# Normalisation statistics of ten feed-forward tiles on ScalarE, and one transpose moved ahead of the MLP's first products

## The chip, the cores and the metric

The kernel runs on one core of one Trainium2 chip. A core has five engines that each run their own list of instructions in order: TensorE (PE in the profile; its weight loads are PEld), VectorE (DVE), ScalarE (ACT), GpSimd (POOL) and SyncE (SP), which issues DMAs. They wait for one another only through semaphores. The metric is the device time of one execution in microseconds, as the median of a few runs; lower is better.

## What is computed

Eight sequences of 256 tokens with 256 features go through one decoder layer: a Mamba block with a gated MLP, an mLSTM cell (the "mixer"), and a feed-forward part whose operands are rounded block by block to a 4-bit grid. Each of the three stands behind a layer norm and a residual. Cut to what the change touches:

```python
def _layernorm(x, axis=-1, eps=1e-05):
    m = jnp.mean(x, axis=axis, keepdims=True)
    v = jnp.var(x, axis=axis, keepdims=True)
    return (x - m) / jnp.sqrt(v + eps)

# Mamba block (inside _L0_attn_ref)
y = y * jax.nn.silu(z)
y = _rms(y, ssm_norm_w)          # x * rsqrt(mean(x*x) + eps) * w
x = x + y @ out_proj_w.T
xn = _rms(x, rms_w)
a, g = jnp.split(xn @ fc1_w.T, 2, axis=-1)
x = x + (a * jax.nn.silu(g)) @ fc2_w.T

# the three sublayers
x = x + _L0_attn_ref(_layernorm(x), ...)
x = x + _L0_xattn_ref(_layernorm(x), ctx, ctx, ...)
x = x + _L0_ffn_ref(_layernorm(x), w_gate, w_up, w_down)

# feed-forward
gate = fp4_linear(x, w_gate)     # quantise x and w in blocks of 16, then matmul
h = jax.nn.silu(gate) * fp4_linear(x, w_up)
out = fp4_linear(h, w_down)
```

## The kernel before

The 2048 rows are 16 tiles of 128 tokens (T = 16), two (C = 2) to each of the B = 8 batches. All work is written out by hand, engine by engine, as lists of stages; a helper `step` calls each stage for the unit that has reached it. Two blocks of code follow each other, `front` (Mamba, MLP, and the query side of the mixer) and `mixer_and_ffn`.

**The front.** A loop over steps k runs with software lags. Two constants matter: SCAN = 9, the step at which the state-space scan starts, and MLP = 18, the step at which the first pair of `fc1` products is issued. Batch numbers in the scan are b = k - SCAN. At k = 18 the scan has only its tail left: batch 7, tile 0 and tile 1 of which still have to be turned (`turn`, four 128x128 transposes on PE into bank 5), copied out by ACT (`turned_y`, line 1151) and projected (`project_out`, line 897). Bank 5 and the target ygT are shared. So `turn(7, 1)` waits for `ygT_ready`, that is, for ACT's `turned_y(7, 0)`. ACT runs `squares` (line 1144, sum of squares with an accumulator) ahead of each `turned_y`, and ahead of both, at k = 18, the two `silu_gate` calls (line 1180) of the first MLP pair. These wait for PE's `fc1` (line 922). `fc1(b, pair)` is 16 weight-load and matmul pairs in the trace (fp32 counts two for each), `fc2` is line 935.

**The feed-forward part.** In `mixer_and_ffn` tile t passes these stages, each at a lag in rounds r:

- ACT `norm(t)` in round t (line 1827, Identity with scale and shift from memory), then DVE's quantiser on x in round t + 1 (lines 320 to 338, tiles xq_*, with ACT's `lift_x`, line 1822, in the middle);
- PE `turn_x` (1701), ACT `turned_x` (1814), PE `gate_up` (1711), ACT `silu` (1808) in round t + 2;
- DVE `product` (1928) and the quantiser on h (tiles hq_*, `lift_h` on ACT, line 1818) in round t + 3;
- PE `turn_h` (1722), ACT `turned_h` (1802, 1803), PE `down` (1730) in round t + 4; DVE `output` (1950) in round t + 5, then the store by SP.

Within a round ACT's order is `turned_x, turned_h, lift_x, lift_h, silu, norm`. PE's is `turn_x, turn_h, gate_up, down`. `gate_up(t)` waits for `turned_x(t)` and for `product(t - 1)`; `product(t)` waits for `silu(t)`. Rounds 0 to 4 are interleaved with the last steps of the mixer; rounds 10 to 15 are a hardware loop of two rounds a pass, on every engine; the others are written out.

**The statistics.** The layer norm ahead of the feed-forward part needs mean and variance of each row. DVE's `row_stats(b)` makes them for both tiles of a batch: two `bn_stats` (line 1918), two `bn_aggr` (line 1922) into `mv`. GpSimd's `row_rstds(b)` makes 1/sqrt(var + eps) and the shift (lines 2027, 2029, 2032), and `norm` waits for that. Batches 0 to 2 are done in mixer steps 4 to 6. Batches 3 to 7 are done between rounds of the feed-forward part: `row_stats(3)` ahead of round 5, and `row_stats(4)` to `row_stats(7)` at the end of rounds 5 to 8.

## Time and profile before

| | us |
|---|---|
| median of 3 runs | 586.91 (586.39 to 587.0) |
| profiled execution, its own time | 588.3 |
| its span, first to last instruction | 586.6 |
| front block | 0 to about 379 |
| mixer, with the first rounds of the feed-forward part from about 415 | 379 to about 450 |
| feed-forward rounds 5 to 15 | about 457 to 554 |
| last rounds | 554 to 586.6 |

The profile is one execution, read by a hardware profiler. For a chain of work that ends late one looks first at which engine has no idle time in a stretch, then at the waits of that engine, then at its rows in order of time. An instruction is pipelined, so that the next one of the same engine often starts about 0.1 us before the end that the row gives; distances between starts are the safer measure. In the last 130 us DVE is nearly without a gap, and in the stretch from 200 to 379 us PE is.

### The profile page before, as it was taken

The page shows a single profiled execution, that of the slowest core. Times are in us where ns is not written, and L with a number is a line of the kernel's source. Part 1 is how long each engine was busy: PE and PEld are TensorE (multiplying, and loading weights), DVE is VectorE, ACT ScalarE, POOL GpSimd, SP SyncE. Part 2 cuts the span into 40 slices and gives each one's busy share as a digit, 9 for nine tenths or more (in the row PEclk, how much of TensorE's full clock was granted, in tenths as well). Part 3 has the DMA queues.
Part 4 walks back from the last instruction along what each step waited for, and adds up shares of the span by engine and source line. Part 5 has one row for each costly group of instructions (what it writes and reads, how often), then busy time and mean ns, then how long its engine had stood idle before and what let it go on. Part 6 is the DMA issues. An engine that isn't in the chain of part 4 may idle for free. (4 is left out here: it accounts for less than half of the span.)

```text
span 586.6 us, 9295 instructions
## 1 busy us (share of the span) xinstructions
PE 559.1 (95%) x3003; PEld 455.6 (78%) x3003; DVE 444.8 (76%) x985; ACT 277.3 (47%) x685; POOL 132.4 (23%) x189
## 2 busy tenths in 40 slices
PE   7999999999999899999999999999997898999995
PEld 6767677689888788888888888878875676777774
DVE  6876799898896234764755856587999999999994
ACT  3876766785796521311111112366874343444431
POOL 4120024454544201211010010007961101000000
PEclk8999999999999999999999999999998899999998
DMA  9300001010000291000000000011000000000000
GB/s 307 128 18 9 29 15 41 7 43 5 6 5 1 87 262 52 1 1 1 0 2 0 1 0 1 4 39 57 19 2 1 10 19 10 18 19 9 18 18 28
DMA packets 21683, 18.94 MB, mean 32 GB/s; under 512 B 12040, under 2 KB 20616, under 8 KB 21256
## 3 DMA queue, kind: packets, MB, share of 16 engines
q1 hardware_dynamic: 21208, 18.36, 9.9%
q8 instruction: 24, 0.39, 0.3%
q14 instruction: 19, 0.16, 0.1%
q10 hardware_dynamic: 432, 0.03, 0.0%
HBM read 16.04 MB, written 2.34 MB: 31 GB/s over the span
## 5 line engine op out<-in xcount | busy, mean ns | idle before, releaser
L922 PE MATMUL ps<-xnT,w_fc 128*128 128x256 f32 x512 | 112.8, 380 | 0.0
L922 PEld LDWEIGHTS ps<-xnT,w_fc 128*128 128x128 f32 x512 | 96.5, 190 | 12.7
L1711 PE MATMUL ps<-w_fc,scores 128*128 128x352 f32 x256 | 81.5, 472 | 3.0 <-issue 3.0
L1711 PEld LDWEIGHTS ps<-w_fc,scores 128*128 128x128 f32 x256 | 48.5, 195 | 29.8 <-issue 5.3
L1180 ACT ACTIVATE xs<-ps 128x512 f32<-128x512 f32 x32 | 19.1, 598 | 95.8 <-PE ps L922 75.7
L1302 DVE SCALAR_TENSOR_TENSOR fold<-xpad,conv_w,fold 128x256 f32<-128x256 f32 x120 | 50.8, 482 | 6.2 <-ACT fold L1082 5.4
L1730 PE MATMUL ps<-u_res,hT 128*128 128x256 f32 x192 | 45.9, 390 | 3.8 <-DVE scores L1950 2.8
L1730 PEld LDWEIGHTS ps<-u_res,hT 128*128 128x128 f32 x192 | 37.5, 196 | 11.9 <-issue 3.0
L799 PE MATMUL ps<-xnT,fold 128*128 128x256 f32 x160 | 39.4, 393 | 1.2 <-ACT xpad L1076 1.2
L799 PEld LDWEIGHTS ps<-xnT,fold 128*128 128x128 f32 x160 | 30.3, 197 | 7.7 <-issue 2.1
L897 PE MATMUL ps<-w_out,xF 128*128 128x256 f32 x128 | 30.4, 381 | 0.8 <-DVE u_res L1401 0.8
L726 POOL TENSOR_SCALAR q_ve<-q_mv 128x2 f32<-128x2 f32 x8 | 1.7, 218 | 129.2 <-DVE q_mv L1426 129.2
L1410 DVE TENSOR_TENSOR fold<-ps,xs 128x512 f32<-128x512 f32 x16 | 11.1, 691 | 26.2 <-ACT xs L1180 26.2
L807 PE MATMUL ps<-fold,xnT 128*128 128x512 f32 x64 | 30.4, 600 | 0.0
L897 PEld LDWEIGHTS ps<-w_out,xF 128*128 128x128 f32 x128 | 23.7, 190 | 7.4 <-issue 4.7
L693 POOL TENSOR_SCALAR_AFFINE_SELECT scores<-scores 128x128 f32<-128x128 f32 x16 | 14.6, 932 | 63.2 <-ACT scores L1110 63.2
L708 POOL TENSOR_TENSOR bc<-xs,head_c 128x512 f32<-128x512 f32 x16 | 25.9, 1623 | 11.8 <-DVE zs L1394 11.8
L935 PE MATMUL ps<-zs,xpad 128*128 128x256 f32 x128 | 28.4, 380 | 0.0
L935 PE MATMUL ps<-zs,fold 128*128 128x256 f32 x128 | 28.3, 379 | 0.0
L935 PEld LDWEIGHTS ps<-zs,fold 128*128 128x128 f32 x128 | 24.3, 190 | 3.3
L935 PEld LDWEIGHTS ps<-zs,xpad 128*128 128x128 f32 x128 | 24.2, 190 | 3.3
L1410 DVE TENSOR_TENSOR xpad<-ps,xs 128x512 f32<-128x512 f32 x16 | 11.1, 692 | 20.1 <-ACT xs L1180 20.1
(305 smaller groups left out, 1202.1 us busy)
## 6 DMA issues: line engine op xcount, KB each, us to landing
zs<-in_ffn_w SPq DMA_DIRECT2D x1, 2112.0 KB, 10.9
x_res<-in_x SPq DMA_DIRECT2D x8, 256.0 KB, 5.8
w_fc<-in_w_fc SPq DMA_DIRECT2D x1, 2048.0 KB, 9.7
xnT<-in_ctxT SPq DMA_DIRECT2D x8, 256.0 KB, 3.1
xs<-in_ctx SPq DMA_DIRECT2D x16, 128.0 KB, 2.9
xs<-in_ctxT SPq DMA_DIRECT2D x8, 256.0 KB, 3.1
out<-scores SPq DMA_DIRECT2D x16, 128.0 KB, 1.7
segs<-segment_rows SPq DMA_DIRECT2D x64, 6.0 KB
```

The costliest lines, as they stand in the source:

```text
L693: last = pool.affine_select(out=tile, in_=tile, pattern=[[1, P]], compare_op=ALU.is_ge, fill=0.0, base=0, channel_multiplier=-1)
L708: pool.tensor_tensor(heads(dx[:, c, :]), heads(m.xs[:, n, :]), inner(m.head_c[:, 2, :], HD), ALU.mult)\
L799: last = pe.matmul(bank[1 + n % 2][:, 0:S], w_in[:, kk, w0:w0 + P], turned_u(b, kk), start=(kk == 0), stop=(kk == KD - 1))
L807: last = pe.matmul(bank[3 + c][:], turned_u(b, kk)[:, c * P:(c + 1) * P], w_in[:, kk, 0:DI], start=(kk == 0), stop=(kk == KD - 1))
L897: last = pe.matmul(bank[6][:, c * D:(c + 1) * D], ygT[:, c, k * P:(k + 1) * P], m.w_out[:, k, :], start=(k == 0), stop=(k == DI // P - 1))
L922: last = pe.matmul(bank[half + r][:, i * S:(i + 1) * S], m.w_fc1[:, kk, col:col + P], m.xnT[:, b, kk * S:(kk + 1) * S], start=(kk == 0), s ...
L935: last = pe.matmul(bank[4 + c][:, 0:D], hid[p][:, k, c * P:(c + 1) * P], w_fc2[:, k, :], start=(k == 0), stop=(k == KM - 1))
L1180: act.activation(gate[:, r, :], bank[2 + r][:], ACT.Silu).then_inc(g["gate_ready"], 1)
L1302: dve.scalar_tensor_tensor(conv[:, p, k, :], xpad[:, p, k, tap:tap + S], m.conv_w[:, ch, tap:tap + 1], conv[:, p, k, :], ALU.mult, ALU.add)\
L1410: dve.tensor_tensor(hid[p][:, 2 * pair:2 * pair + 2, :].rearrange("p k t -> p (k t)"), bank[r][:], gate[:, r, :], ALU.mult).then_inc(g["hi ...
L1711: last = pe.matmul(bank[1 + j][:, 0:HALF], xT[:, p, k * P:(k + 1) * P], m.w_gu[:, k, j * HALF:(j + 1) * HALF], start=(k == 0), stop=(k == ...
L1730: last = pe.matmul(bank[7][:, 0:D], hT[:, p, k, :], m.w_dn[:, k, :], start=(k == 0), stop=(k == KF - 1))
```

## The change

It has two parts that don't touch each other.

**In the front,** at step 18, `turn(7, 0)` is issued on PE ahead of `fc1(0, 0)` and `fc1(0, 1)`; on ACT `squares(7, 0)` and `turned_y(7, 0)` stand ahead of `silu_gate(0, 0)` and `silu_gate(0, 1)`. The argument `n=B - 1` keeps the old place for batches 0 to 6.

**In the feed-forward part,** batches 3 to 7 lose `row_stats` on DVE. ACT gets a `row_stats(t)` for one tile, called for t = r + 2 at the end of rounds 4 to 13. It makes two passes over the 256 elements of a row: Identity with scale 1/256, whose accumulator is the mean, and Square of (mean - x), whose accumulator is 256 times the variance; between the two it waits for its own first pass. GpSimd multiplies by 1/256 where it adds eps, in one instruction as before. ACT's rounds 10 to 15 are no longer a loop but written out.

```diff
@@ front, PE
+            if k == MLP:
+                turn(B - 1, 0)
             on(fc1, k - MLP, 0)
             on(fc1, k - MLP, 1)
-            on(turn, b - 2, 0)
+            on(turn, b - 2, 0, n=B - 1)
@@ front, ACT
+            if k == MLP:
+                squares(B - 1, 0)
+                turned_y(B - 1, 0)
             on(silu_gate, k - MLP, 0)
             on(silu_gate, k - MLP, 1)
-            on(squares, b - 2, 0)
-            on(turned_y, b - 2, 0)
+            on(squares, b - 2, 0, n=B - 1)
+            on(turned_y, b - 2, 0, n=B - 1)
@@ feed-forward, ACT
+        def row_stats(t):
+            b, mean, square_sum = t // C, mv[:, t, 0:1], mv[:, t, 1:2]
+            act.wait_ge(s["x2_ready"], LEAD + C * (b + 1))
+            act.wait_ge(f["f_mv_ready"], LEAD + b)
+            scrap = sq[:].rearrange("p i e -> p (i e)")[:, 0:D]
+            act.activation(scrap, m.x_res[:, t, :], ACT.Identity, scale=1.0 / D, accum_out=mean)\
+               .then_inc(f["f_stats"], 1)
+            act.wait_ge(f["f_stats"], LEAD + STATS_BY_DVE + t + 1 - C * STATS_BY_DVE)
+            last = act.activation(scrap, m.x_res[:, t, :], ACT.Square, bias=mean, scale=-1.0, accum_out=square_sum)
+            if t % C == C - 1:
+                last.then_inc(f["f_mv_ready"], 1)
...
-        rounds(act, forward, 4)
+        for r in range(4, T + depth_of(forward)):
+            step(T, forward, r)
+            if C * STATS_BY_DVE <= r + 2 < T:
+                row_stats(r + 2)
@@ feed-forward, DVE
-            if 4 <= k <= B - 2:
+            if 4 <= k < 4 + STATS_BY_DVE:
                 row_stats(k - 4, k % 2)
...
-        row_stats(3, 1)
-        for r in range(5, 9):
-            step(T, forward, r)
-            row_stats(r - 1, (r - 1) % 2)
-        rounds(dve, forward, 9)
+        rounds(dve, forward, 5)
@@ feed-forward, GpSimd
-            pool.tensor_scalar(ve[:, here], mv[:, here, 1], LN_EPS, None, ALU.add).then_inc(f["f_ve_ready"], 1)
+            pool.tensor_scalar(ve[:, here], mv[:, here, 1], share, LN_EPS, ALU.mult, ALU.add)\
+                .then_inc(f["f_ve_ready"], 1)
```

PE in the front at step 18, the difference between the two kernels (L907 is `turn_xn`, L888 `turn`, L922 `fc1`, L897 `project_out`; fp32 matmuls count once here):

```order
 L897 MATMUL ps<-w_out,xF 128x256 x4
 L907 MATMUL ps<-ident,fold 128x128 x4
+L888 MATMUL ps<-ident,zs 128x128 x4
 L922 MATMUL ps<-xnT,w_fc 128x256 x16
-L888 MATMUL ps<-ident,zs 128x128 x8
+L888 MATMUL ps<-ident,zs 128x128 x4
 L897 MATMUL ps<-w_out,xF 128x256 x8
 L922 MATMUL ps<-xnT,w_fc 128x256 x8
```

The two turnings stood together behind the products; now one stands ahead of them.

ACT at the same step, before (L1172 is `turned_xn`, L1180 `silu_gate`, L1144 `squares`, L1151 `turned_y`):

```order
233 L1172 ACTIVATE xnT<-ps,rms_w 128x256 x2
234 L1180 ACT_TABLE_LOAD
235 L1180 ACTIVATE xs<-ps 128x512 x2
236 L1144 ACTIVATE xF,ms<-zs 128x512
237 L1151 ACTIVATE xF<-ps 128x512
238 L1144 ACTIVATE xF,ms<-zs 128x512
239 L1151 ACTIVATE xF<-ps 128x512
```

and now (two lines further down in the file):

```order
233 L1174 ACTIVATE xnT<-ps,rms_w 128x256 x2
234 L1146 ACTIVATE xF,ms<-zs 128x512
235 L1153 ACTIVATE xF<-ps 128x512
236 L1182 ACT_TABLE_LOAD
237 L1182 ACTIVATE xs<-ps 128x512 x2
238 L1146 ACTIVATE xF,ms<-zs 128x512
239 L1153 ACTIVATE xF<-ps 128x512
```

`squares` and `turned_y` of tile 0 now run ahead of the table load and the two silu calls.

ACT in one feed-forward round, before (L1814 `turned_x`, L1802 and L1803 `turned_h`, L1822 `lift_x`, L1818 `lift_h`, L1808 `silu`, L1827 `norm`):

```order
331 L1814 ACTIVATE scores<-ps 128x256
332 L1802 ACTIVATE hT<-ps 128x512
333 L1803 ACTIVATE hT<-ps 128x256
334 L1822 ACTIVATE xq_g<-xq_g,grid_bias 128x256
335 L1818 ACTIVATE hq_g<-hq_g,grid_bias 128x704
336 L1808 ACTIVATE sg<-ps 128x704
337 L1827 ACTIVATE scores<-x_res,f_shift,f_rstd 128x256
```

and now (six lines further down; L1842 and L1845 are the two passes):

```order
333 L1820 ACTIVATE scores<-ps 128x256
334 L1808 ACTIVATE hT<-ps 128x512
335 L1809 ACTIVATE hT<-ps 128x256
336 L1828 ACTIVATE xq_g<-xq_g,grid_bias 128x256
337 L1824 ACTIVATE hq_g<-hq_g,grid_bias 128x704
338 L1814 ACTIVATE sg<-ps 128x704
339 L1833 ACTIVATE scores<-x_res,f_shift,f_rstd 128x256
340 L1842 ACTIVATE scores,f_mv<-x_res 128x256
341 L1845 ACTIVATE scores,f_mv<-x_res,f_mv 128x256
342 L1820 ACTIVATE scores<-ps 128x256
```

The two passes stand between `norm` and the next round's `turned_x`, with no table load among them.

## Rows read from the trace of the kernel before

**Rows 1.** Page, part 1: busy us, share of the span and instructions of each engine.

```profile
PE 559.1 (95%) x3003; PEld 455.6 (78%) x3003; DVE 444.8 (76%) x985; ACT 277.3 (47%) x685; POOL 132.4 (23%) x189
```

**Rows 2.** Busy time by stretch: PE, PEld, DVE, ACT, POOL, then PE clock, DMA.

```profile
215.00:370.00 155.00, 155.00 (x759) 136.96 (x758) 96.23 (x203) 28.43 (x57) 17.75 (x25) 1.00 0.05 12
```

**Rows 3.** PE's waits, 200 to 385 us: total us, times, longest.

```profile
PE ps L888 <- ACT xF L1151: 1.7, 1, 1.7
```

**Rows 4.** Timeline of step 18: start, duration, engine, line, operation [idle before <-releaser].

```profile
190.86 7.07 PE L922 MATMUL ps<-xnT,w_fc 128*128 128x256 f32 x32
...
194.56 1.28 ACT L1180 ACT_TABLE_LOAD   x1 [2.66 <-PE ps L922]
...
197.77 0.60 PE L888 MATMUL ps<-ident,zs 128*128 128x128 f32 x4
198.03 0.60 ACT L1180 ACTIVATE xs<-ps 128x512 f32<-128x512 f32 x1 [1.58 <-PE ps L922]
198.52 0.62 ACT L1144 ACTIVATE xF<-zs 128x512 f32<-128x512 f32 x1
...
199.33 0.60 ACT L1151 ACTIVATE xF<-ps 128x512 f32<-128x512 f32 x1
...
200.07 0.63 PE L888 MATMUL ps<-ident,zs 128*128 128x128 f32 x4 [1.70 <-ACT xF L1151]
...
200.53 3.62 PE L897 MATMUL ps<-w_out,xF 128*128 128x256 f32 x16
```

**Rows 5.** Busy time by stretch, one round each, with and without DVE statistics.

```profile
486.75:496.11 9.36, 8.46 (x36) 6.15 (x36) 9.04 (x24) 3.83 (x8) 1.45 (x5) 1.00 0.04 15
...
512.97:521.41 8.44, 8.35 (x37) 5.93 (x36) 8.15 (x19) 3.80 (x8) 0.00 (x0) 1.00 0.05 17
```

**Rows 6.** Timeline of DVE at the end of round 8: the statistics of batch 7.

```profile
494.39 0.75 DVE L1918 BATCH_NORM_STATS2 f_st<-x_res 128x6 f32<-128x256 f32 x2
...
495.17 0.25 DVE L1922 BATCH_NORM_AGGREGATE f_mv<-f_st 128x2 f32<-128x6 f32 x2
495.33 0.86 DVE L1928 TENSOR_TENSOR hf<-ps,sg 128x704 f32<-128x704 f32 x1
```

**Rows 7.** Timeline of a looped round without statistics, PE, ACT and DVE.

```profile
517.97 2.75 PE L1730 MATMUL ps<-u_res,hT 128*128 128x256 f32 x12
518.17 0.76 ACT L1808 ACTIVATE sg<-ps 128x704 f32<-128x704 f32 x1 [0.68 <-PE ps L1711]
...
518.83 0.59 ACT L1827 ACTIVATE scores<-x_res,f_shift,f_rstd 128x256 f32 x1
...
520.56 0.38 PE L1701 MATMUL ps<-ident,scores 128*128 128x128 f32 x2
520.61 0.89 DVE L1928 TENSOR_TENSOR hf<-ps,sg 128x704 f32<-128x704 f32 x1
...
521.06 0.39 ACT L1814 ACTIVATE scores<-ps 128x256 f32<-128x256 f32 x1 [1.64 <-PE ps L1701]
...
521.72 4.90 PE L1711 MATMUL ps<-w_fc,scores 128*128 128x352 f32 x16
...
529.46 0.39 ACT L1814 ACTIVATE scores<-ps 128x256 f32<-128x256 f32 x1 [1.48 <-PE ps L1701]
```

**Rows 8.** Timeline of ACT in the MLP: two accumulating passes, then a scaled copy.

```profile
240.14 0.41 ACT L1158 ACTIVATE fold<-u_res 128x256 bf16<-128x256 f32 x1
...
240.68 0.42 ACT L1158 ACTIVATE fold<-u_res 128x256 bf16<-128x256 f32 x1
...
241.09 0.89 ACT L1165 ACTIVATE fold<-u_res,rs 128x256 f32<-128x256 f32 x2
```

**Rows 9.** Round 5: busy time and PE clock of 1 us, then timeline.

```profile
461.00:462.00 1.00, 1.00 (x3) 0.62 (x2) 1.00 (x3) 0.11 (x1) 0.00 (x0) 0.50 0.00 0
...
458.88 6.67 PE L1711 MATMUL ps<-w_fc,scores 128*128 128x352 f32 x16 [0.89 <-issue]
...
465.58 0.76 ACT L1808 ACTIVATE sg<-ps 128x704 f32<-128x704 f32 x1 [2.37 <-PE ps L1711]
...
467.27 0.86 DVE L1928 TENSOR_TENSOR hf<-ps,sg 128x704 f32<-128x704 f32 x1
```

More of the change, by code:

```diff
@@ L1564, in mixer_and_ffn @@
     LATER = B // 2
+    STATS_BY_DVE = 3
     chain = GateChain(m, 1, lambda name, shape: sb(name, shape)[:])
@@ L2025, in row_rstds @@
             here = slice(C * b, C * (b + 1))
+            share = 1.0 if b < STATS_BY_DVE else 1.0 / D
             pool.wait_ge(f["f_mv_ready"], LEAD + b + 1)
-            pool.tensor_scalar(ve[:, here], mv[:, here, 1], LN_EPS, None, ALU.add).then_inc(f["f_ve_ready"], 1)
+            pool.tensor_scalar(ve[:, here], mv[:, here, 1], share, LN_EPS, ALU.mult, ALU.add)\
+                .then_inc(f["f_ve_ready"], 1)
             pool.wait_ge(f["f_ve_ready"], LEAD + b + 1)
```

## The prediction, made before the changed kernel ran

> **What bounds the kernel now.** I read four views. The busy shares come first: PE 95%, DVE 76%, ACT 47% [rows 1]. They are an average over stages with different limits, so the second view is busy time by stretch. From 215 to 370 us PE is busy all 155 of 155 us [rows 2], and DVE and ACT have plenty of room. There, only what PE doesn't have to wait for can shorten the time. The third view is PE's waits. Between 200 and 385 us they hold one real wait: `turn(7, 1)` for ACT's copy `turned_y(7, 0)`, 1.7 us [rows 3]. In the feed-forward rounds the picture turns: in a round of 8.44 us DVE is busy 8.15 us, and the rest is one wait of some 0.3 us for ACT's lift. A round with statistics takes 9.36 us, with 9.04 us of DVE [rows 5]. So DVE sets the pace there, and PE is close behind with 8.35 of 8.44 us.
>
> **Part 1, the turning.** Before, PE issues `turn(7, 0)` at 197.77, can't issue `turn(7, 1)` before 200.07, and goes on to `project_out` at 200.53 [rows 4]. A turning costs 200.53 - 200.07 = 0.46 us of PE. So the gap between the two is 2.30 us, of which 0.46 is work and 1.84 is waiting. ACT causes it: it is busy with the second silu at 198.03, then `squares` at 198.52, then `turned_y` at 199.33 [rows 4]. After the change `turn(7, 0)` goes out at 190.86 and its copy runs on ACT while PE works through 32 matmuls of `fc1`. ACT has 2.66 us idle there [rows 4]. `squares` and `turned_y` take 0.81 + 0.60 = 1.41 us, by the distance 198.52 to 199.33 and the duration of the second.
>
> What is late next? `fc1` and all behind it move down by 0.46 us. Then `turn(7, 1)` starts at 198.23 without a wait, and `project_out(7, 0)` at 198.69. It is half of 3.62 us, so PE wants tile 1 at 200.50. ACT does the second silu at 198.49, `squares(7, 1)` 0.49 later at 198.98, `turned_y(7, 1)` at 199.79, done at 200.39; PE reacted 0.14 us after such an end before (199.33 + 0.60 to 200.07), so 200.53. That costs 0.03, at most 0.1 us. The first silu stands behind the table load of 1.28 us as before [rows 4], 0.46 later, and the next `fc1` pair starts some 5 us after it. Nothing else in the front is gated by time: the loads of w_fc2 and the feed-forward weights are issued behind `turn(7, 1)` and `squares(7, 1)`, hence 0.9 us or so earlier instead of 1.8, but the first `fc2` is over 20 us away. **Gain 1.8 us** (1.7 to 1.84), and with PE full up to 370 us it goes through to the end of the front [rows 2, 3]. From below: if the wait only moved to `project_out`, the gain would be nothing.
>
> **Part 2, DVE's side.** One `row_stats(b)` takes from 494.39 to 495.33 = 0.94 us of DVE [rows 6], and the round lengths say 9.36 - 8.44 = 0.92 us [rows 5]. Five of them go: one ahead of round 5, four in rounds 5 to 8. 5 x 0.92 = **4.6 us** if DVE stays the bound.
>
> **Part 2, ACT's side.** Ten tiles get two passes each. No row shows exactly these, but two squares with an accumulator over 256 elements stand in the MLP: the second starts 0.54 us after the first, with the wait for its own semaphore between, and the next instruction 0.41 us after that [rows 8]. The second pass takes its bias from memory. `norm`, with both bias and scale from memory, takes 0.59 where the square takes 0.41 [rows 7, 8], so 0.09 for each; I add one. A tile then costs 0.54 + 0.41 + 0.09 = 1.04 us. The upper bound is that each pass costs as much as `norm` plus a read of the accumulator, which I estimate from these rows at 0.2 us: 2 x 0.79 = 1.6 us, and 0.1 for the wait: 1.7 us. The lower bound is two bare passes without the read, 0.8 us. I take 1.04, since the same pattern with the same width stands in the trace.
>
> The cover is ACT's idle time between `norm` and the next `turned_x`, which waits for PE's `turn_x`: 1.64 us in one round and 1.48 in the next [rows 7]. So 1.04 us fits with 0.4 us left, and 1.7 us doesn't: it would push `turned_x` by 0.2. Behind the passes are queued `turned_x`, `turned_h` and the lifts; PE waits for the first of these to start `gate_up`. If the cover were gone, all of it would fall on PE and, PE having almost no spare time, on the end. In rounds 5 to 8 the idle time was longer only because the round was; without DVE's statistics they look like the looped rounds.
>
> The two waits added ahead of the passes are long satisfied: x_res is complete by about 451 us. The other way round, tile t's `norm` needs the statistics of its batch by way of GpSimd. Tile 7's come at the end of round 5, about 466 us, GpSimd takes under 2 us, and `norm(6)` runs about 8 us later. The unrolling of ACT's loop I cost at nothing, as DVE waits for ACT only at the lift. GpSimd's second operand costs nothing: the same single instruction.
>
> The ScalarE page of the Trainium skill (ScalarE: Activation LUTs, Rules for kernel authors) speaks against this part: plain adding and multiplying belongs on VectorE, not on ScalarE. In engine time the row agrees with it: 2 x 1.04 us of ACT replace 0.93 of DVE. By that rule the five batches would be 5.8 us more work for 0 gain; the sum goes by who ends the round, and that is DVE.
>
> **PE's speed in round 5.** The granted clock is at its lower level, 1.2 GHz, around 461 us (0.50), after a stretch in which PE waited for DVE, and `gate_up(3)` takes 6.67 us where a later one takes 4.90 [rows 7, 9]. Its silu ends at 466.34 and `product` starts at 467.27, so 0.93 us were free [rows 9]. The change pulls `product` forward by two statistics, 1.84 us, and `gate_up` by one (0.92), because it starts behind the previous `product`. So 0.93 - 0.92 = nothing is left, and with reaction time about **0.1 us** is lost. Later rounds run at full speed and PE regains some 0.05 us a round.
>
> **The sum.** 1.8 + 4.6 - 0.1 = 6.3 us. The profiled span goes from 586.6 to 580.3 us. The profiled execution took 588.3 us, 1.7 us more than its span; the median of the unprofiled runs is 586.91, and I take the same 6.3 us from that: **580.6 us**.
>
> **The rivals.**
>
> - *PE takes over in the feed-forward part* (0.10). For it: PE is busy 8.35 of 8.44 us [rows 5], and at the lower clock `gate_up` takes 1.8 us more [rows 9]. If such a stretch falls into a round that has no slack, most of 1.3 us stays. Against: rounds 16 and the looped ones run at 8.44 with the same PE work. 580.6 + 1.3 = 581.9.
> - *ACT overruns its gap* (0.08). At 1.7 us a tile the push is up to 0.2 us in ten rounds, 2 us: 582.6.
> - *The front's wait only moves* (0.05). If `project_out(7, 1)` or a later silu eats the 1.8 us: 582.4.
> - *Slower than before* (0.02). One mechanism: the pair of passes is so dear that ACT ends the round. It decides from 1.48 us on. To eat 6.3 us over ten tiles it must cost 1.48 + 0.63 = 2.1 us. That is far above 1.04, but it would be reached if the passes and silu needed different tables: two loads of 1.28 us a round [rows 4] make 1.04 + 2.56 = 3.6 us, 2.1 over the gap, 21 us in ten rounds, and 602 us. Against: Square follows silu without a load at 198.52 [rows 4], Identity at 518.83 [rows 7]. The same page of the Trainium skill (What ACT_TABLE_LOAD costs) puts a switch of tables at about 2.7 us with a drain; with that instead of 1.28 it would be some 630 us.
>
> **How the numbers follow.** The forecast holds 0.75, at 580.6 with 580.1 to 581.1 of its own. The cases of a smaller gain lie at 581.9 to 582.6, together 0.23. The range reaches 579.8, in case the reaction times are kinder, and 582.5. A measurement of this kernel can tell about 0.2%, 1.2 us, from no change. All cases but the last and a failure of both parts (0.02) are faster by more than that: faster 0.96, same 0.02, slower 0.02.
>
> **What the changed profile would show.** Step 1: PE's wait ahead of the transpose at about 198 us is gone, `project_out` starts at 198.7, and the front ends 1.8 us sooner. Step 2: starts of `product` are 8.44 us apart from round 5 on. Step 3: the two passes start 0.54 us apart, `turned_x` starts at once behind `turn_x`, and ACT still has about 0.4 us idle ahead of it. Step 4: in round 5 DVE waits 0.1 us for silu. The forecast is wrong if ACT's `turned_x` starts without an idle time before it, or if DVE shows waits for PE or silu in rounds 6 to 15.

## The result, and the profile after

The changed kernel took 583.37 us (median of 10 executions, 580.97 to 585.14), the kernel before 587.0 us beside it (586.39 to 588.65): ratio 0.9928, 95% interval 0.9914 to 0.9943. That is 4.2 us faster by the ratio. The forecast was 6.3 us and 580.6 us, and 583.37 lies outside its range, on the side of the smaller gain. The profiled execution took 583.46 us with a span of 581.7 us, 4.9 under the span of before (586.6).

The page's first part (busy us, share and instructions of each engine) answers to [rows 1]:

```profile
PE 558.2 (96%) x3003; PEld 454.3 (78%) x3003; DVE 441.2 (76%) x965; ACT 287.2 (49%) x725; POOL 133.5 (23%) x189
```

Twenty instructions left DVE and forty (20 passes, 20 reads of the accumulator) came to ACT, ten times 1.0 us of its time. POOL has the same number of instructions and 1.1 us more of them. That last figure turned out to be the one that matters.

**The front.** PE's waits of 190 to 385 us of the changed kernel (total us, times, longest), which answers to [rows 3]; `L888`'s 1.7 us is gone:

```profile
PE ps L1650 <- PEq L224: 0.7, 1, 0.7
```

Timeline of step 18 of the changed kernel, which answers to [rows 4]:

```profile
190.88 0.60 PE L888 MATMUL ps<-ident,zs 128*128 128x128 f32 x4
...
191.32 7.07 PE L922 MATMUL ps<-xnT,w_fc 128*128 128x256 f32 x32
...
195.02 1.28 ACT L1182 ACT_TABLE_LOAD   x1 [1.80 <-PE ps L922]
...
198.23 0.60 PE L888 MATMUL ps<-ident,zs 128*128 128x128 f32 x4
...
198.66 3.96 PE L897 MATMUL ps<-w_out,xF 128*128 128x256 f32 x16
198.98 0.62 ACT L1146 ACTIVATE xF<-zs 128x512 f32<-128x512 f32 x1
...
199.79 0.60 ACT L1153 ACTIVATE xF<-ps 128x512 f32<-128x512 f32 x1
...
202.47 0.81 PE L922 MATMUL ps<-xnT,w_fc 128*128 128x256 f32 x3
```

All starts are where the forecast put them, to 0.03 us. But `project_out`'s 16 matmuls take 3.96 us where they took 3.62: a pause of 0.34 us stands inside the group, behind tile 0's half, for the copy that ends at 200.39.

**The rounds.** Starts of VectorE's `product` (timeline, DVE), which answer to the round lengths of [rows 5]:

```profile
457.31 0.89 DVE L1949 TENSOR_TENSOR hf<-ps,sg 128x704 f32<-128x704 f32 x1
465.74 0.89 DVE L1949 TENSOR_TENSOR hf<-ps,sg 128x704 f32<-128x704 f32 x1
474.17 0.89 DVE L1949 TENSOR_TENSOR hf<-ps,sg 128x704 f32<-128x704 f32 x1
482.61 0.89 DVE L1949 TENSOR_TENSOR hf<-ps,sg 128x704 f32<-128x704 f32 x1
```

They are 8.43 or 8.44 apart, and so are all from round 5 to the product of tile 8; three later distances are longer, 8.71 once and 8.47 twice (below). One such round on ScalarE (timeline, ACT with its neighbours), which answers to [rows 7, 8]:

```profile
480.82 0.59 ACT L1833 ACTIVATE scores<-x_res,f_shift,f_rstd 128x256 f32<-128x256 f32 x1
481.32 0.40 ACT L1842 ACTIVATE scores<-x_res 128x256 f32<-128x256 f32 x1
...
481.62 0.19 ACT L1842 ACTIVATION_READ_ACCUMULATOR scores<-x_res 128x1 f32 x1
...
481.84 0.51 ACT L1845 ACTIVATE scores<-x_res,f_mv 128x256 f32<-128x256 f32 x1
482.26 0.19 ACT L1845 ACTIVATION_READ_ACCUMULATOR scores<-x_res,f_mv 128x1 f32 x1
...
482.98 0.39 ACT L1820 ACTIVATE scores<-ps 128x256 f32<-128x256 f32 x1 [0.53 <-PE ps L1707]
```

The second pass starts 0.52 after the first, the pair is over 1.13 us after its start, and 0.53 us of idle time is left: the forecast had 0.54, 1.04 and 0.4.

**What the forecast didn't have.** In the mixer's last steps GpSimd makes the reciprocal deviations `rv`, which VectorE waits for, and then `row_rstds` of batches 0 to 2, with the new multiplication. Timeline of POOL in the kernel before, batch 0 (L2027 is `f_ve`, L2029 `f_rstd`, L2032 `f_shift`):

```profile
409.06 1.65 POOL L2009 TENSOR_TENSOR rv<-var,minus_half 128x8 f32<-128x8 f32 x1
410.69 0.22 POOL L2027 TENSOR_SCALAR f_ve<-f_mv 128x2 f32<-128x2 f32 x1
410.99 1.02 POOL L2029 TENSOR_TENSOR f_rstd<-f_ve,minus_half 128x2 f32<-128x2 f32 x1
412.11 0.51 POOL L2032 TENSOR_SCALAR f_shift<-f_mv,f_rstd 128x1 f32<-128x1 f32 x2
```

and of the changed kernel, with the product on DVE that `rv` releases:

```profile
408.25 1.65 POOL L2026 TENSOR_TENSOR rv<-var,minus_half 128x8 f32<-128x8 f32 x1
409.93 0.69 DVE L1925 TENSOR_TENSOR scores<-scores,rv 128x512 f32<-128x512 f32 x1
409.98 0.69 POOL L2045 TENSOR_SCALAR f_ve<-f_mv 128x2 f32<-128x2 f32 x1
410.75 0.70 POOL L2048 TENSOR_TENSOR f_rstd<-f_ve,minus_half 128x2 f32<-128x2 f32 x1
411.55 0.50 POOL L2051 TENSOR_SCALAR f_shift<-f_mv,f_rstd 128x1 f32<-128x1 f32 x2
```

The instruction that was forecast to cost nothing takes 0.69 instead of 0.22 us, and from `rv`'s end to the first `f_shift` it is 1.65 instead of 1.40 us. That is 0.25 us, and batch 1 loses 0.20 in the same way. Most of the loss, 0.71 us, comes in batch 2, where `f_ve` itself is short again. The changed kernel there, POOL and DVE:

```profile
423.93 0.19 POOL L2045 TENSOR_SCALAR f_ve<-f_mv 128x2 f32<-128x2 f32 x1
424.21 1.27 POOL L2048 TENSOR_TENSOR f_rstd<-f_ve,minus_half 128x2 f32<-128x2 f32 x1
...
427.83 1.25 DVE L328 TENSOR_SCALAR xq_g<-xq_v 128x256 int32<-128x256 int32 x1
...
430.98 0.69 DVE L1925 TENSOR_TENSOR scores<-scores,rv 128x512 f32<-128x512 f32 x1 [0.35 <-POOL rv L2026]
```

`f_rstd` took 0.71 us before. On VectorE L328 took 0.29 and L326 ahead of it 0.97, which is 0.41 now, so the two are 0.40 us longer together. Both engines' work there is longer than before, and VectorE waits 0.35 us for `rv` at the sixth product, where it didn't wait before.

**Where the 4.9 us of the two spans come from**, by the same five marks in both traces (VectorE's first row behind the front, its first and sixth product with `rv`, `product` of tiles 1 and 3, and the end):

| stretch | before | after | difference |
|---|---|---|---|
| start to VectorE's first row behind the front | 379.57 | 378.04 | -1.53 |
| to the first product with `rv` | 18.81 | 19.54 | +0.73 |
| to the sixth | 32.26 | 33.40 | +1.14 |
| to `product` of tile 1 | 15.80 | 15.79 | 0 |
| to `product` of tile 3 | 20.83 | 18.97 | -1.86 |
| to the end | 119.33 | 115.96 | -3.37 |

The second row is TensorE's clock (the third, 1.14 us, is the 0.25, 0.20 and 0.71 us of the three batches to 0.02). Busy time by stretch, the changed kernel, with PEclk behind the bracketed counts:

```profile
380.00:381.00 1.00, 1.00 (x4) 0.58 (x3) 0.86 (x5) 1.00 (x4) 0.00 (x0) 0.50 0.00 0
```

The granted clock is 0.50, that is 1.2 GHz, from 378.2 to 381.6 us, behind a wait of 0.7 us, and the first 16 products of queries and keys (L1667) take 2.68 us where the next take 2.10. Before, that stretch ran at 2.4 GHz although the same wait of 0.7 us stood ahead of it, so the wait alone doesn't decide it; but the kernel before had such a stretch at 575 to 579 us, which the changed one doesn't have, and this is 1.0 of the last row's 3.37.

### The profile page after: what moved, and what is told of

It is laid out like the page before. It is cut to its first block and busy times, and to the rows that moved or that the text cites. A ratio compares the mean times of both kernels' runs of the same rounds, so it can differ in the third digit from the quotient of the medians.

```text
span 581.7 us, 9282 instructions
## 1 busy us (share of the span) xinstructions
PE 558.2 (96%) x3003; PEld 454.3 (78%) x3003; DVE 441.2 (76%) x965; ACT 287.2 (49%) x725; POOL 133.5 (23%) x189
## 5 line engine op out<-in xcount | busy, mean ns | idle before, releaser
L922 PE MATMUL ps<-xnT,w_fc 128*128 128x256 f32 x512 | 112.8, 380 | 0.0
L922 PEld LDWEIGHTS ps<-xnT,w_fc 128*128 128x128 f32 x512 | 96.5, 190 | 12.7
L1717 PE MATMUL ps<-w_fc,scores 128*128 128x352 f32 x256 | 80.0, 466 | 0.0
L1736 PE MATMUL ps<-u_res,hT 128*128 128x256 f32 x192 | 44.2, 380 | 3.8 <-DVE scores L1971 2.8
L1736 PEld LDWEIGHTS ps<-u_res,hT 128*128 128x128 f32 x192 | 36.3, 190 | 11.3 <-issue 3.0
L799 PE MATMUL ps<-xnT,fold 128*128 128x256 f32 x160 | 38.0, 382 | 1.2 <-ACT xpad L1078 1.2
L807 PE MATMUL ps<-fold,xnT 128*128 128x512 f32 x64 | 31.7, 621 | 0.0
L897 PE MATMUL ps<-w_out,xF 128*128 128x256 f32 x128 | 30.6, 382 | 0.9 <-DVE u_res L1406 0.8
L897 PEld LDWEIGHTS ps<-w_out,xF 128*128 128x128 f32 x128 | 23.6, 190 | 7.8 <-issue 5.2
```

The source lines that it names most:

```text
L799: last = pe.matmul(bank[1 + n % 2][:, 0:S], w_in[:, kk, w0:w0 + P], turned_u(b, kk), start=(kk == 0), stop=(kk == KD - 1))
L807: last = pe.matmul(bank[3 + c][:], turned_u(b, kk)[:, c * P:(c + 1) * P], w_in[:, kk, 0:DI], start=(kk == 0), stop=(kk == KD - 1))
L897: last = pe.matmul(bank[6][:, c * D:(c + 1) * D], ygT[:, c, k * P:(k + 1) * P], m.w_out[:, k, :], start=(k == 0), stop=(k == DI // P - 1))
L922: last = pe.matmul(bank[half + r][:, i * S:(i + 1) * S], m.w_fc1[:, kk, col:col + P], m.xnT[:, b, kk * S:(kk + 1) * S], start=(kk == 0), s ...
L1717: last = pe.matmul(bank[1 + j][:, 0:HALF], xT[:, p, k * P:(k + 1) * P], m.w_gu[:, k, j * HALF:(j + 1) * HALF], start=(k == 0), stop=(k == ...
L1736: last = pe.matmul(bank[7][:, 0:D], hT[:, p, k, :], m.w_dn[:, k, :], start=(k == 0), stop=(k == KF - 1))
```

## The experiments

**A measure for executions of different clocks.** In every trace of this study the clock is low in stretches of 3.4 us (the expectations say 3.5 to 4), one, two or three of them in a row, each of which leaves 1.7 us less of full-speed time than its length, or 0.003 of the mean clock. Most stand in a few places that repeat (98, 377 to 388, 443 to 453, 567 to 583 us; single ones at 9, 43 and 459), and an execution has one to six of them. So I compare spans at equal mean clock, and, in the traces, the distances between marks. Medians of the spans in us, by the mean granted clock of the execution, of all executions whose clock was recorded, with their number (two of the kernel before, of 1471 and 3269 us, and all with a clock under 0.988 are left out):

| kernel | clock 0.997 | 0.994 | 0.991 | 0.988 |
|---|---|---|---|---|
| before | 584.2 (3) | 585.2 (16) | 586.5 (19) | 586.5 (10) |
| front_only | 582.4 (2) | 583.4 (8) | | |
| stats_only | | 582.2 (1) | 582.0 (4) | 583.6 (2) |
| pool_only | | | 586.1 (6) | 587.3 (4) |
| the changed kernel, twice | 579.4 (2) | 580.6 (7) | 581.6 (3) | 583.0 (1) |
| pool_split, twice | 578.1 (5) | 579.3 (3) | 580.8 (1) | 581.3 (1) |
| later_rstd | 578.6 (2) | 579.9 (2) | 581.0 (1) | 582.8 (1) |
| both_turned, twice | 577.9 (2) | 579.3 (1) | 580.0 (4) | 581.1 (4) |
| dve_unrolled | | 578.6 (1) | 579.6 (3) | 580.9 (1) |

The measure is coarse. Many cells hold one or two executions, and those of the kernel before at 0.991 lie between 584.5 and 587.2 us. Most distances between marks repeat to 0.1 us from trace to trace, those that the clock moves aside, and where the two differ I go by the marks.

**front_only**: the kernel before with the first part of the change alone.

> The kernel before with the front's part of the change alone (turn(7, 0), squares(7, 0), turned_y(7, 0) ahead of the first products; statistics untouched). The changed kernel's trace shows the step at 202.47 us instead of 203.99, so 1.5 us gained at that point. Theory G (GpSimd: the loss behind the front comes from the two-operand instruction in row_rstds): the 1.5 us go through to the end, 585.5 against 587.0. Theory C (clock: the loss comes from a stretch at TensorE's lower clock at the start of the second block): a gain of 0.8 to 1.5 us, with a wide spread between executions, and a lower clock in the stretch behind 378 us in those that are slow.

585.25 us, ratio 0.9959 (0.9942 to 0.9976), and 1.8 us less at equal clock (584.2 to 582.4, 585.2 to 583.4). Its `f_ve` rows are those of before, 0.22 us each, and its marks from the first to the sixth product are 32.26 us apart. So the front's gain reaches the end, and the loss of 1.14 us doesn't come from the front's arriving earlier.

**stats_only**: the second part alone, with its change on GpSimd.

> The kernel before with the statistics' part of the change alone, GpSimd's edit with it. Forecast on record for this part: 4.6 us. Theory G: 4.6 - 1.2 = 3.4 us gained, 583.6 us, since x goes to the same GpSimd instructions between 408 and 432 us. Theory C: 4.5 us gained but for chance, 582.5 us.

584.01 us, ratio 0.995 (0.9926 to 0.9974), nearer to theory G than to C. The first product stands 33.38 us ahead of the sixth, `f_ve` takes 0.69, 0.69 and 0.19 us. `product` comes every 8.43 us from tile 2 to tile 8.

**pool_split**: the changed kernel, with the old instruction where the share is 1.

```
-            pool.tensor_scalar(ve[:, here], mv[:, here, 1], share, LN_EPS, ALU.mult, ALU.add)
+            if b < STATS_BY_DVE:
+                pool.tensor_scalar(ve[:, here], mv[:, here, 1], LN_EPS, None, ALU.add)
+            else:
+                pool.tensor_scalar(ve[:, here], mv[:, here, 1], 1.0 / D, LN_EPS, ALU.mult, ALU.add)
```

> The changed kernel, but GpSimd adds eps for batches 0 to 2 with the old one-operand instruction, and multiplies by 1/256 only for batches 3 to 7. Theory G: the 1.1 us lost between 409 and 431 us come back, median 582.2 against 583.4 of the changed kernel, and f_ve takes 0.2 us again at about 410 us. Theory C: no difference, 583.4 us.

**pool_only**: the kernel before with only the new form, `1.0, LN_EPS, ALU.mult, ALU.add`.

> The kernel before, with nothing changed but GpSimd's instruction: times 1.0 and plus eps instead of plus eps, for all batches. Theory G: slower by about 1.1 us (588.1 us), all of it between 409 and 431 us. Theory C and the forecast (a second operand costs nothing): no difference, 587.0 us.

pool_split: ratio 0.9892 (0.9855 to 0.9929), 580.57 us, and the marks are 32.23 us apart again. pool_only: 588.47 us, ratio 1.0021 (1.0001 to 1.0041), marks 33.41. The table at equal clock doesn't show its loss (586.1 against 586.5 at 0.991, 587.3 against 586.5 at 0.988), because the cells of the kernel before are that wide; a pair of traces does. pool_only and two_adds (below) have low stretches in the same places but for one more of pool_only near 450 us, their first row behind the front is at 378.09 and 378.10 us and their first product at 396.91 and 396.93, the sixth is at 430.32 and 429.14, and the spans are 586.1 and 585.0. So the loss reaches the end. With front_only and stats_only, the kernels make a square: 33.4 wherever the new form is in the first three batches, 32.2 to 32.3 wherever it isn't, with the front and the statistics changed or not. The loss of 1.14 us belongs to this instruction, and taking it back makes a better kernel. The first run of pool_split was thin (6 executions, two of them at a clock of 0.982), so it was run once more.

> The changed kernel with GpSimd's old one-operand instruction for the three batches whose sums of squares need no scaling, once more, as the kernel that the next is held against. Theory G+C (in the traces so far VectorE's sixth product with the reciprocal deviations comes 32.24 us behind the first with one operand and 33.38 to 33.41 with two, whatever else is changed): 32.2 again, spans of 578.1 to 578.3 at a mean clock of 0.997 and 579.3 at 0.994, 0.9 to 1.3 us under the changed kernel at the same clock. Rival (the first run of it was lucky): equal to the changed kernel at equal clock.

Ratio 0.9898 (0.9874 to 0.9921), 580.8 us, spans of 578.0 and 578.1 at 0.997 and 579.1 in the middle at 0.994. The changed kernel's repeat:

> The changed kernel once more, as the kernel that the others of this set are held against. Theory C (the spread between executions is TensorE's granted clock: in the traces so far every low stretch is 3.5 to 4 us at a granted clock near 0.5 and takes 1.7 us of full-speed time, which is 0.003 of the mean clock): spans of 579.1 at a mean clock of 0.997, 580.2 to 580.9 at 0.994, 581.5 to 581.7 at 0.991, 583 at 0.988, so that two executions of equal mean clock agree within 0.7 us and one low stretch more costs 0.8 to 1.2 us. Rival (the spread has another cause): executions of equal mean clock differ as much as executions of different clocks, 2 us or more.

Ratio 0.9928 (0.9902 to 0.9954), and spans of 579.7 at 0.997, 580.2 to 581.2 at 0.994, 584.5 at 0.982. For the changed kernel theory C holds: equal clock, equal time, within 1.0 us. For the kernel before it doesn't in full: its 19 executions at 0.991 spread over 2.7 us, as the rival said. The mean clock isn't the whole, and the place of the low stretches counts too. The repeat's profiled execution has no low stretch in the front or at 378 us, though the same wait of 0.7 us stands there, and its marks show it: the front ends at 376.29 us instead of 378.04, and the first product with `rv` comes 18.82 us behind that instead of 19.54. The places have prices of their own. One stretch in the front costs 1.5 to 1.75 us (unchanged fronts end at 378.0 to 378.3 without, 379.6 to 379.8 with one; changed ones at 376.3 to 376.8 and 377.6 to 378.1). Behind the front the first costs 0.7 and each further one 1.5 (18.82, 19.54, 21.0 and 22.51 us with none, one, two, three). Near 575 us one costs 0.9 to 1.1, and two in a row 2.35 (both_turned). Between 443 and 453 it costs nothing that the marks show, since VectorE carries those rounds.

**two_adds and one_mult**: what in the new form makes it late? Both are the kernel before, with `LN_EPS, 0.0, ALU.add, ALU.add` (two operands, nothing multiplied) and with `1.0, None, ALU.mult` (one operand, multiplied). Each ran once, with the profiler, so they are read by their marks and rows alone.

> The kernel before, with GpSimd's instruction adding 0.0 as a second operand behind the addition of epsilon, in all eight batches: nothing is multiplied. Theory G2 (it is the second operand that lets VectorE's product start first: with it the instruction starts 0.08 us behind rv's end, with one operand 0.02 us ahead of it): 0.69 us, 0.69 us and 0.19 us in the first three batches, and the sixth product 33.4 us behind the first. Rival M (it is the multiplication): 0.22 us in each and 32.25 us.

> The kernel before, with GpSimd's instruction multiplying by 1.0 in place of adding epsilon, one operand: epsilon is left out of this variance. Theory G2: 0.22 us in each batch and the sixth product 32.25 us behind the first. Rival M: 0.69, 0.69 and 0.19 us and 33.4 us.

I had expected the second operand to be the cause, and it isn't. The theory G2 fell in both. Timeline of POOL and DVE, two_adds:

```profile
407.59 1.65 POOL L2009 TENSOR_TENSOR rv<-var,minus_half 128x8 f32<-128x8 f32 x1
409.22 0.23 POOL L2027 TENSOR_SCALAR f_ve<-f_mv 128x2 f32<-128x2 f32 x1
409.27 0.69 DVE L1904 TENSOR_TENSOR scores<-scores,rv 128x512 f32<-128x512 f32 x1
```

and one_mult:

```profile
411.54 1.65 POOL L2009 TENSOR_TENSOR rv<-var,minus_half 128x8 f32<-128x8 f32 x1
413.22 0.69 DVE L1904 TENSOR_TENSOR scores<-scores,rv 128x512 f32<-128x512 f32 x1
413.27 0.73 POOL L2027 TENSOR_SCALAR f_ve<-f_mv 128x2 f32<-128x2 f32 x1
```

Behind `rv` (a power), an instruction that adds starts 0.02 us ahead of `rv`'s modelled end and one that begins with a multiplication 0.08 us behind it. VectorE's product with `rv` starts 0.03 us behind it. So the adding one is ahead of VectorE's and takes 0.22, and the multiplying one is behind it and ends 0.05 to 0.09 us after it. The later start is there in the third batch too, where the instruction isn't held: 0.09 us behind `rv`'s end in the changed kernel, 0.02 ahead of it in two_adds. In that batch the power behind `f_ve` is held (1.27 us, against 0.71). That GpSimd's instruction has to wait for something that VectorE's holds is the plain reading of starts and ends; these runs don't take VectorE's product away, so it is argued, not shown. What is shown is that the form that begins with a multiplication costs 1.14 us (33.41 and 33.46 us in pool_only and one_mult) and a second addition nothing (32.21 in two_adds). An instruction that adds first and then multiplies wasn't tried.

**later_rstd**: if GpSimd carries that stretch, taking `row_rstds(2)` out of it should gain.

```
-            if k < B:
-                on(row_rstds, k - 5, (k - 5) % 2)
+            if 5 <= k < B - 1:
+                row_rstds(k - 5, (k - 5) % 2)
+            if k == B + 1:
+                row_rstds(2, 0)
```

> GpSimd's one-operand instruction for the first three batches, and the reciprocal deviations of the third batch taken out of GpSimd's stretch of 424 to 426 us and put behind those of the last batches but one, where GpSimd idles 3.9 us in the changed kernel's trace (before 440.52). Theory G (GpSimd carries the end of the mixer between 408 and 431 us): the stretch loses the 1.6 us from f_ve to the second f_shift of that batch; VectorE's own work there has 0.8 us of waits to give, so 0.3 to 1.0 us less than the kernel with the one-operand instruction (spans of 577.2 to 578.0 at a mean clock of 0.997, 578.3 to 579.0 at 0.994). Rival D (VectorE carries that stretch): the same time as without the move, within 0.2 us at equal clock.

It gained nothing: 581.73 us, ratio 0.9914 (0.989 to 0.9938), 0.2 to 1.5 us more than pool_split at equal clock, first to sixth product 32.37 us, and 16.24 instead of 15.8 from there to `product` of tile 1. Theory G was half right. In pool_split's repeat `rv` of the sixth ends at 425.71 + 1.69 = 427.40 and VectorE starts on it at 427.44, straight from its own work: the two engines reach that point together. So what makes GpSimd later is paid. That making it earlier brings nothing isn't shown by this run, since it hardly made it earlier: GpSimd now waits 1.13 us for VectorE's product and 0.45 for ScalarE, and the sixth `rv` ends 32.14 us behind the first product, against 32.20. VectorE lost besides: its L322 takes 1.02 us beside GpSimd's earlier instruction, and 0.23 in pool_split's repeat. Rival D, that VectorE carries that stretch, fits as far as these rows go.

**act_twice**: the cover of the passes on ScalarE.

```
+            for i in range(2):
+                act.activation(spare[:, t % 2, i, :], m.x_res[:, t, :], ACT.Identity, scale=1.0 / D,
+                               accum_out=extra[:, t, i:i + 1])
             act.activation(scrap, m.x_res[:, t, :], ACT.Identity, scale=1.0 / D, accum_out=mean)
```

> The changed kernel with two more plain accumulating passes a tile on ScalarE whose results nobody reads, ahead of the two that the statistics need: 2 x 0.53 = 1.06 us more of ScalarE a round in ten rounds. ScalarE idles 0.53 us behind the present pair in a looped round, so turned_x comes 0.5 us later. Theory V (VectorE alone sets the round of 8.43 us; its product has 1.7 us of room behind silu): the round stays at 8.43 and the time is that of the changed kernel within 0.5 us at equal clock. Rival P (TensorE has hardly any room left: 0.38 + 0.84 + 4.97 + 2.6 us of its own in a round, one behind the other): gate_up starts 0.3 to 0.5 us later and the round grows to 8.7 to 8.9, 3 to 5 us in all.

582.68 us, ratio 0.9922 (0.9904 to 0.994), rounds of 8.43 us as before, 580.3 to 581.2 at a clock of 0.994 and 580.2 to 580.5 at 0.991 (the changed kernel: 580.2 to 581.2, and 581.5 to 581.7): no loss. Timeline of its round, PE, ACT and DVE:

```profile
492.61 0.40 ACT L1845 ACTIVATE spare<-x_res 128x256 f32<-128x256 f32 x1
...
493.01 0.40 ACT L1845 ACTIVATE spare<-x_res 128x256 f32<-128x256 f32 x1
...
493.41 0.40 ACT L1847 ACTIVATE scores<-x_res 128x256 f32<-128x256 f32 x1
...
493.91 0.88 DVE L1954 TENSOR_TENSOR hf<-ps,sg 128x704 f32<-128x704 f32 x1
...
494.45 0.36 ACT L1822 ACTIVATE scores<-ps 128x256 f32<-128x256 f32 x1
...
494.89 0.53 PE L1719 MATMUL ps<-w_fc,scores 128*128 128x352 f32 x1
```

Passes that wait for nothing start 0.40 apart, so two are 0.80 and not 1.06 us. All of the idle time is used up, `turned_x` starts 0.54 behind `product` instead of 0.38, and `gate_up` 0.98 behind it instead of 0.99. The 0.16 us don't reach it, since it stands behind `turn_h` anyway.

**filled**: TensorE kept busy in its wait of 4.4 us ahead of round 2's transposes (base: pool_split).

```
         turn_down(2)
+        for _ in range(9):
+            pe.matmul(bank[0][:], m.ident[:], m.w_gu[:, 0, 0:512], start=True, stop=True)
```

> GpSimd's one-operand instruction for the first three batches, and nine matmuls of 512 columns whose result nobody reads, put on TensorE behind the last turning of the down weights, where TensorE waits 4.4 us for round 2's hidden rows (441.7 to 446.1 us in the changed kernel). They leave the computation as it is. Theory C1 (the low stretch of clock at 445 to 450 us, which all six traces so far show, follows that wait): the stretch is gone from the trace, the mean clock is 0.003 higher, and gate_up of round 2 takes 5.0 us at full clock where a part of it ran at half; the time falls by 0 to 0.9 us, by 0 where VectorE alone carries those rounds. Rival C2 (the low stretches fall where they like): one still stands between 440 and 465 us, and the mean clock is as without them.

Each took 0.88 us, twice what I had reckoned, so the transpose behind them, which stands 0.66 us ahead of tile 1's `product` in the changed kernel (446.11 and 446.77), stands 3.22 behind it here (448.92 and 445.70): 3.9 us late. It is the one trace of seventeen without a low stretch between 440 and 460 us, which speaks for C1, and its mean clock is no higher: two others stand at 377 to 383 us. `product` of tiles 1 and 2 are 10.54 us apart as in the changed kernel all the same. So the rounds there have room on TensorE, and neither filling nor the low clock moves VectorE's rounds. In time it was 583.15 us, ratio 0.9921 (0.9902 to 0.9939), and 0.9 us over pool_split at 0.994 (2 against 3 executions). A likely reason, not shown, is that a low stretch near 446 us costs nothing, so that at equal mean clock this kernel has more of those that cost.

**both_turned**: the pause inside `project_out` taken away, by turning the second tile early as well, on TensorE between the two `fc1` and on ScalarE between the two silus (base: pool_split).

```
                 turn(B - 1, 0)
             on(fc1, k - MLP, 0)
+            if k == MLP:
+                turn(B - 1, 1)
             on(fc1, k - MLP, 1)
```

> The kernel with one operand for the three batches, and batch 7's second tile turned ahead of the second product pair of the first MLP step too (TensorE's turning, ScalarE's squares and copy), since its gated values are ready at 190.0 us and it is turned at 196.5 to 198.2. Theory W (what the front's forecast of 1.8 us lost is the wait of project_out(7, 1) for that copy, 0.3 us): the wait goes and VectorE's first batch statistics behind the front (378.0 in the changed kernel's trace, 376.3 in its repeat) come 0.3 us earlier at equal clock, the spans 0.3 us shorter, 577.8 to 578.0 at a mean clock of 0.997. Rival X (ScalarE, which sits with a table load between the two gates, is made later): silu's second gate comes 1.0 us later, the second fc1 sums wait for nothing, and the time is the same or up to 0.5 us longer.

> The kernel with one operand for the three batches and both of batch 7's tiles turned early, once more. By the sums so far: spans of 577.6 to 577.8 at a mean clock of 0.997, 578.6 to 579.0 at 0.994, 579.6 to 580.5 at 0.991, and a ratio to the kernel before of 0.9885 to 0.990. If it is no better than the kernel without the second early turning: 578.1, 579.1 and 580.8 at these clocks.

Timeline of PE in both_turned:

```profile
189.17 0.60 PE L907 MATMUL ps<-ident,fold 128*128 128x128 f32 x4
...
193.50 0.60 PE L888 MATMUL ps<-ident,zs 128*128 128x128 f32 x4
...
197.40 3.62 PE L897 MATMUL ps<-w_out,xF 128*128 128x256 f32 x16
200.85 0.38 PE L922 MATMUL ps<-xnT,w_fc 128*128 128x256 f32 x1
```

`project_out` is back at 3.62 us, and from L907 to the next `fc1` it is 11.68 us against 12.02 in the changed kernel: the 0.34 us are gained there, so the cause of the pause is shown. The second silu starts 8.49 us behind L907 instead of 8.04, so rival X is right on its direction, and nothing waits for it. The front of both_turned didn't end 0.3 us sooner, though: 376.42 against 376.38 in pool_split's repeat, because this execution was 0.39 us later at 189 us already. At equal clock the spans say 0.2 us at 0.997, nothing at 0.994, 0.8 at 0.991, from few executions. Ratios: 0.9905 (0.9879 to 0.9931) and 0.9882 (0.9858 to 0.9906).

**act_unrolled and dve_unrolled**: 0.40 us of the looped rounds. In the ten traces with the statistics on ScalarE and VectorE's loop in place, `product` of tiles 8 and 9 are 8.70 or 8.71 apart and two later pairs 8.46 to 8.48 (two, not the three that the first of the expectations below names); with the statistics on VectorE all are 8.43. The edits: ScalarE's rounds written out in the kernel before; VectorE's rounds written out in both_turned.

> The kernel before, with ScalarE's last rounds written out as the changed kernel has them, in place of its loop, and nothing else. Theory U (ScalarE written out meets VectorE's loop differently, and that costs 0.40 us: products of tiles 8 and 9 are 8.71 us apart and three later pairs 8.47): the same pattern here. Rival L (it comes with the statistics' absence from VectorE, whose instructions then stand elsewhere): 8.43 or 8.44 throughout behind the rounds with statistics, as before.

> The kernel with one operand for the three batches and with both of batch 7's tiles turned early, and VectorE's loop of rounds written out too. Theory L2 (VectorE's loop costs the 0.40 us: 0.28 where it is entered, 0.04 at each return): all rounds 8.43 apart, and 0.4 us less than both_turned at equal clock (177.2 us left behind the front's end would be too fine to tell; the starts of the products tell it). Rival (the code written out has to be fetched and costs more than the loop): one or more gaps over 8.5 us, and the time the same or longer.

act_unrolled (one execution) has 8.41 to 8.44 behind the rounds with statistics, so ScalarE's written-out rounds alone don't do it. dve_unrolled has 8.43 throughout: from `product` of tile 1 to that of tile 15 it is 119.26 us, against 119.63 in both_turned and 119.69 in the changed kernel. Timeline of DVE in round 11, the second round of its loop's first pass, in the changed kernel:

```profile
507.91 0.89 DVE L1949 TENSOR_TENSOR hf<-ps,sg 128x704 f32<-128x704 f32 x1
508.71 0.41 DVE L320 TENSOR_REDUCE xq_amax<-scores 128x16 f32<-128x256 f32 x1
509.31 0.89 DVE L320 TENSOR_REDUCE hq_amax<-hf 128x44 f32<-128x704 f32 x1 [0.18 <-issue]
```

and in dve_unrolled:

```profile
506.57 0.88 DVE L1954 TENSOR_TENSOR hf<-ps,sg 128x704 f32<-128x704 f32 x1
507.37 0.41 DVE L320 TENSOR_REDUCE xq_amax<-scores 128x16 f32<-128x256 f32 x1
507.69 0.87 DVE L320 TENSOR_REDUCE hq_amax<-hf 128x44 f32<-128x704 f32 x1
```

The two reductions are 0.60 us apart in the first and 0.32 in the second. The engine waits for nothing that the profile shows there. The expectation puts the 0.28 us at the entry of the loop; the entry is round 10, with the product of tile 7, and costs nothing. All three longer rounds, 11, 13 and 15, are the second of a pass. Why the same loop costs nothing in the kernel before stays open; its instructions stand at other places of the program, and that wasn't varied. dve_unrolled: ratio 0.9883 (0.9859 to 0.9906), and 0.4 us under both_turned at 0.991 (579.6 and 580.0). Both runs of pool_split, both of both_turned and the one of dve_unrolled have lower ratios than the changed kernel's 0.9928. Three kernels (pool_split, both_turned, dve_unrolled) beat both, being 1.0 to 1.2% under the kernel before where the changed one is 0.7% under it. Between the last two the measurement can't tell.

## Why the prediction was wrong

- **Part 1, the turning: the mechanism right, 1.8 us a little high.** The wait of 1.84 us went. The forecast gave `project_out(7, 1)` "0.03, at most 0.1 us"; it waits 0.34. Two sizes were off, both in when TensorE goes on with tile 1. The 16 matmuls of 3.62 us follow each other every 0.216 us ((3.62 - 0.38) / 15), so tile 1 was wanted at 198.66 + 8 x 0.216 = 200.39 and not at 200.50. And the copy ended at 200.39, as reckoned, but work went on at 200.73, 0.34 behind it, where the forecast took the 0.14 that a transpose had needed. From L907 to the next `fc1` the change brings 13.57 - 12.02 = 1.55 us. At the front's end it is 1.53 (both traces with a low stretch in the front), 1.7 by the medians of the traces without one (378.0 to 378.3 against 376.3 to 376.8), 1.8 by the spans of front_only.
- **Part 2, VectorE's statistics: 5 x 0.92 = 4.6 right.** Products 11.48 to 10.54 and four times 9.35 to 8.43: 4.6 us. What the forecast lacked is the 0.40 us that VectorE's loop then costs in the later rounds, so 4.2 are left. It took the length of a round without statistics from looped rounds of the kernel before, and took it that these would stay as they are; three of them got longer.
- **Part 2, ScalarE's side: right.** 1.04 us forecast, 1.13 to the last read's end, and 0.53 us idle left where 0.4 was said. act_twice shows that even 0.80 more would have cost nothing, so the rival in which ScalarE overruns was further away than its 0.08 says. The rule on plain arithmetic (the Trainium skill, ScalarE: Activation LUTs, Rules for kernel authors) is borne out as engine time, 1.0 us of ScalarE a tile for 0.46 of VectorE, and not as time of the kernel.
- **GpSimd's second operand: the step that failed.** "GpSimd's second operand costs nothing: the same single instruction" put at nothing a term that is 1.14 us, shown by kernels with and without it. It is the multiplication, not the number of operands. The instruction by itself is the same length (0.19 to 0.23 where it isn't held). I costed it by its duration and didn't look at who is queued behind it: VectorE waits for `rv`, GpSimd makes the next `rv` behind this instruction, and in the kernel without the loss the two reach the sixth within 0.04 us of each other. A row for this stood in the trace of before: `f_rstd` takes 1.02 and 1.14 us in the first two batches and 0.71 in the third, one operation of one shape, so its form alone didn't set its length. It isn't simply whether VectorE works: in the third batch a product of VectorE's starts 0.08 us behind `f_rstd`'s start (424.59 and 424.51) and it takes 0.71, in the changed kernel 0.01 behind (424.22 and 424.21) and it takes 1.27. Which of the two starts first looks decisive, and that isn't shown. No rival covered the term.
- **TensorE's clock.** The 0.1 us of round 5 didn't occur, as the low stretch at 459 us wasn't there, and where one stands at 443 to 453 us it costs nothing. The forecast took the low stretches of one trace as part of the kernel. They move from execution to execution, and one in the front or behind it costs 0.7 to 1.75 us, more than most terms that were argued over.

The sum as it stands: front 1.5 to 1.8, statistics 4.6, less 1.14 for the multiplication and 0.40 for the loop, makes 4.6 to 4.9 us. At equal clock the spans say 4.8 (584.2 to 579.4), 4.6 (585.2 to 580.6) and 4.9 (586.5 to 581.6). Two of the terms that were missed, 1.14 and 0.40, and 0.1 to 0.3 of the front are the difference to 6.3. The ratio gives 4.2 and the two medians 3.6; what lies between those and 4.8 is most likely the clock that the executions happened to get (the ten of the changed kernel have 0.982 to 0.997; for the ten of the kernel before beside it none is on record).

No rival was the case. The time lies above all three cases of a smaller gain (581.9, 582.6 and 582.4 us), and none of them happened: VectorE waits for nothing new in the rounds, ScalarE keeps 0.53 us idle, and the front keeps at least 1.5 us of its gain.

## What to carry to other kernels

An edit to a small instruction on a side engine is costed by what is queued behind it and who waits for that, not by its own length; where two engines reach a meeting point together, a delay on either is paid, and a gain on one alone can't be counted on. If the same small operation has several durations in the trace, something beside it may set them, and a change of its form or start can cost a microsecond. And before two traces are compared, their clocks are: compare executions of equal mean granted clock, and better the distances between marks, since a low stretch costs nothing in one place and 1.75 us in another.

## What the runs showed of the hardware

- On GpSimd, behind a power of 128x8, an instruction that multiplies first started 0.10 us later than one that adds (0.08 behind the power's end against 0.02 ahead of it); the number of operands made no difference (0.22 and 0.23 us with one and two additions).
- A GpSimd instruction on 128x2 that started 0.05 us behind a VectorE product of 128x512 took 0.69 to 0.73 us instead of 0.22 and ended 0.05 to 0.09 us behind it. Started 0.04 us behind a VectorE product of 128x256 that reads `ps` (PSUM), it took 0.19 (changed kernel, 423.93 us).
- An accumulating pass of ScalarE over 256 columns takes 0.40 us (0.51 with the bias from memory) and 0.19 for the read of the accumulator, and such passes follow each other every 0.40 us.
- The granted clock falls to 1.2 GHz for 3.4 us at a time, in one to six stretches of a trace, in places that repeat but aren't all taken each time. Some stand behind pauses of TensorE (0.7 us ahead of 378, 4.4 ahead of 446), but the changed kernel's repeat has the same pause of 0.7 us and no fall there, and at 98 us it fell although TensorE had been busy all of 90 to 98. A stretch costs between nothing (443 to 453 us) and 1.75 us (in the front).
- A loop of VectorE, two rounds a pass, cost 0.28 us in the second round of its first pass and some 0.04 in that of the two others, in kernels whose last ten tiles have their statistics on ScalarE, and nothing in those that have them on VectorE.
